# Two chunked scans: the step scaling of the turned channels given to ScalarE, and the first scan's gate moved ahead of the carry

## What is computed

```python
def step(h, inp):                       # per position t and head (16 heads of 64 channels)
    h = h * dA_t + (dt_t * x_t) * B_t   # dt: the step, one number per position and head
    return h, einsum('bhpn,bn->bhp', h, C_t)
y = ys + D_param * xh                   # the skip
y = y * silu(z)                         # the gate
y = y * rsqrt(mean(y * y) + 1e-5) * rms_w ; return y @ out_proj_w.T
```

## Time and profile before

| | us |
|---|---|
| median of 3 runs | 4476.42 (4476.28 to 4478.08) |
| the profiled execution | 4481.21 |
| its span in the profile | 4479.5 |
| TensorE busy in the span | 4064.1 (91%) |
| VectorE busy | 3152.3 (70%) |
| ScalarE busy | 1652.2 (37%) |
| GpSimd busy | 1034.0 (23%) |

### The profile page before, as it was taken

One profiled execution on the slowest core, in us unless ns is written; L12 is line 12 of the kernel. 1 busy time (PEld: TensorE's weight loads), 2 busy tenths in 40 slices (PEclk: granted clock), 3 DMA queues, 4 the chain that ended last, 5 costly groups with the idle time before them and its releaser, 6 DMA issues. The chain is left out here.

```text
span 4479.5 us, 71612 instructions
## 1 busy us (share of the span) xinstructions
PE 4064.1 (91%) x26200; PEld 3023.7 (68%) x26200; DVE 3152.3 (70%) x6457; ACT 1652.2 (37%) x3472; POOL 1034.0 (23%) x597
## 2 busy tenths in 40 slices
PE   6999999998799999999778888898898799999999
PEld 5767676765566666666466676576576478787877
DVE  5787878774489999899657647657557566666664
ACT  3434343432333333343237537447357311111111
POOL 0333434343055555555500000000000000000000
PEclk8999999999899999999889999999999899999999
DMA  2110111001201111111143142242341310101000
GB/s 107 37 37 29 38 42 39 28 35 39 86 26 51 44 39 45 51 44 37 40 175 100 62 142 84 92 134 62 117 126 50 121 34 24 34 22 36 27 26 19
DMA packets 150049, 266.40 MB, mean 59 GB/s; under 512 B 30276, under 2 KB 36424, under 8 KB 149704
## 3 DMA queue, kind: packets, MB, share of 16 engines
q1 hardware_dynamic: 149704, 261.83, 17.5%
HBM read 164.88 MB, written 88.34 MB: 57 GB/s over the span
## 5 line engine op out<-in xcount | busy, mean ns | idle before, releaser
L1866 DVE TENSOR_REDUCE xa_mn<-xa_s 128x1 f32<-128x896 f32 (+7 forms) x512 | 373.0, 751 | 135.8 <-PE xa_s L1961 134.8
L1781 ACT ACTIVATE xa_src<-xa_s,xa_mn 128x896 f32<-128x896 f32 (+7 forms) x512 | 377.7, 740 | 231.6 <-DVE xa_mn L1866 230.3
L1967 PE MATMUL xa_gen<-xa_ident,xa_src 128*128 128x128 f32 x2304 | 310.2, 278 | 53.3 <-ACT xa_pT L1790 26.3
L73 PE MATMUL ff_wb<-ff_w_hi,ff_st_hi 128*128 128x512 f32 x768 | 323.8, 422 | 10.4 <-DVE ff_parts L2472 10.4
L940 DVE SCALAR_TENSOR_TENSOR mb_cv<-mb_xc,mb_cw,mb_cv 128x256 f32<-128x256 f32 x432 | 310.8, 773 | 31.9 <-ACT mb_xc L746 27.8
L1728 POOL TENSOR_TENSOR xa_res<-xa_res,xa_bor 128x512 f32<-128x512 f32 x32 | 40.5, 1270 | 1244.7 <-DMA xa_res<-after_mamba_dram 1244.7
L74 PE MATMUL ff_wb<-ff_w_hi,ff_st_lo 128*128 128x512 f32 x768 | 311.9, 406 | 0.0
L75 PE MATMUL ff_wb<-ff_w_lo,ff_st_hi 128*128 128x512 f32 x768 | 311.1, 405 | 0.0
L1967 PEld LDWEIGHTS xa_gen<-xa_ident,xa_src 128*128 128x128 f32 x2304 | 251.1, 143 | 75.1 <-ACT xa_src L1781 59.5
L1309 PE MATMUL mb_ib<-mb_wc,mb_yT 128*128 128x512 f32 x512 | 262.6, 661 | 1.8 <-DVE mb_y L1078 1.0
L2240 POOL TENSOR_TENSOR ff_mixed<-ff_at,ff_rw 128x1024 f32<-128x1024 f32 x32 | 60.9, 1904 | 875.3 <-DVE ff_at L2500 875.3
(11 more groups left out here) (494 smaller groups left out, 11031.7 us busy)
## 6 DMA issues: line engine op xcount, KB each, us to landing
xa_qa<-xa_q_dram SPq DMA_DIRECT2D x384, 64.0 KB, 2.0
xa_q_dram<-xa_kq SPq DMA_DIRECT2D x32, 512.0 KB, 2.8
xa_k_dram<-xa_kq SPq DMA_DIRECT2D x32, 512.0 KB, 2.8
xa_ka<-xa_k_dram SPq DMA_DIRECT2D x192, 64.0 KB, 2.0
xa_st<-xa_k_dram SPq DMA_DIRECT2D x192, 64.0 KB, 2.0
mf_xg<-in_x_dram SPq DMA_DIRECT2D x16, 512.0 KB, 5.1
turned_dram<-mf_xt_hi SPq DMA_DIRECT2D x16, 512.0 KB, 2.7
turned_dram<-mf_xt_lo SPq DMA_DIRECT2D x16, 512.0 KB, 4.0
```

The source lines that it names most:

```text
L73: nc.tensor.matmul(out, w_hi, x_hi, start=first, stop=False)
L1781: a_.activation(pq[:, hh, 0:w], s1[g, i, hh][:, 0:w], ACT.Exp, scale=-1.0, bias=mn[:, i % 2, hh:hh + 1], accum_out=sums[:, i // QT, i % QT ...
L1866: v_.tensor_reduce(mn[:, i % 2, hh:hh + 1], s1[g, i, hh][:, 0:(i + 1) * P], AX.X, ALU.min).then_inc(mx_ready.sem, 1)
L1967: last = tr(ps[:, n * P:(n + 1) * P], pq[:, hh, j * P:(j + 1) * P], ident[:])
```

## The change

In both scans GpSimd's product of `xtok` and the steps goes away. A new step `scaled` on ScalarE makes `xdt` with one operation per head, sixteen per chunk, each 128 x 64 with the head's step as a per-partition scale. It stands right behind `turn` and ahead of `front` or of the rest of `back`. GpSimd's skip product now waits for it. In the first scan's even turns `gate` comes ahead of `carry`.

```diff
                 if 0 <= n - 1 < N:
                     yield "turn", n - 1
+                if 0 <= n + 1 < N:
+                    yield "scaled", n + 1
                 if n % 2 and 0 <= (n + 3) // 2 < NGF:
                     yield "front", (n + 3) // 2
...
                 if -1 <= n < N:
                     yield "mixed", n
+                if -1 <= n < N and not backward and n % 2 == 0:
+                    yield "gate", n
                 if 0 <= n < N:
                     yield "carry", n
...
-                if -1 <= n < N:
+                if -1 <= n < N and (backward or n % 2):
                     yield "gate", n
...
             def inputs(c):
                 (r, t), b = ring(c), c % 2
-                wait(pool, dt_ready, c // GT)
...
-                g_.tensor_tensor(heads(xdt[:, b]), heads(xtok[:, b]), bcast(dt[:, r, t, :], 2, HP), ALU.mult)\
-                    .then_inc(xdt_ready.sem, 1)
                 wait(pool, xdt_ready, c)
                 g_.tensor_tensor(heads(xtok[:, b]), heads(xtok[:, b]), bcast(dsk[:], 2, HP), ALU.mult).then_inc(skip_ready.sem, 1)
...
+            def scaled(c):
+                (r, t), b = ring(c), c % 2
+                wait(act, dt_ready, c // GT)
+                if backward:
+                    wait(act, dt_loaded[c // GT % 2], c // GT // 2)
+                wait(act, xtok_ready, 2 * c + 1)
+                wait(act, intra_full, NQ * (c - 1) - 1)
+                if c >= 2:
+                    wait(act, xw_ready, outer(c - 2) - int(final(c - 2)))
+                if c == 1:
+                    act.wait_ge(half_ready, 2 * KD)
+                for h in range(NH):
+                    cols = slice(h * HP, (h + 1) * HP)
+                    last = a_.activation(xdt[:, b, cols], xtok[:, b, cols], ACT.Identity, scale=dt[:, r, t, h:h + 1])
+                last.then_inc(xdt_ready.sem, 1)
```

More of the change, by code:

```diff
@@ L858, in _ @@
             run({"split": split, "consts": consts, "combine": combine, "xT": turn_in, "front": front, "back": channels, "sums": sums, "inputs": inputs,
-                 "turn": turn, "square": square, "tanh": front_tanh, "silu": silu, "mixed": mixed, "output": output})
+                 "turn": turn, "scaled": scaled, "square": square, "tanh": front_tanh, "silu": silu, "mixed": mixed, "output": output})
         @block.vector
```

## The result

The changed kernel takes 4497.47 us (median of six runs, 4486.17 to 4499.47), the kernel before 4478.09 on the same chip: a ratio of 1.004 [1.0027, 1.0053]. So the change costs 19 us: slower, as forecast, but by half of the 38 us that were forecast. The profiled execution of the changed kernel took 4497.97 us, 16.8 more than that of before.

What follows compares the result with a forecast made beforehand. The scans were taken as bound by TensorE's work plus its stalls. +91 - 22 - 33 - 28 + 30 = +38 us on the profiled 4481.2 gave 4519, and 4514 as median of runs; range 4450 to 4576.

Steps and rivals of the forecast that it cites:

- The new operations: ScalarE's sixteen scaled operations: 354 ns each, one starting every 0.25 us, 4.0 us put into its turn, bounds 2.6 and 5.7.
- +91: Both scans: TensorE's first z product waits for ScalarE's bank copies, 2.27 or 2.23 us in even turns, 0.8 in odd.
- +121 and -83: Forecast losses, +91 for z product stalls and +30 for clock, against savings of 22 (gate), 33 (state) and 28 (clock).
- The gate: First scan, even turns: gate ahead of carry ends the transposes' 24.4 us wait, about 2.4 returning as later state: -22 us.
- The state: Second scan: without GpSimd's product the taps shorten, VectorE waits for TensorE, state waits fall to 0.74 each: -33 us.
- The clock: Half speed behind the second scan's long stalls goes, -28 us; the new 2.2 to 2.3 us stalls cost +30 us.
- I take half: Clock loss behind the 30 new even-turn stalls, 2 us each: none makes 0, all make 60, so +30 us.
- The even exchange: Rival: the new 2.2 us z product stalls don't lower the clock; +8 us, 4484, counted as no change; chance 0.17.
- VectorE stays late: Rival: second scan's taps don't shorten, so the 33 and 28 us don't come back; +99 us, 4575; chance 0.05.
- Dear operations: Rival: ScalarE's operations don't overlap, 5.7 us put in, stalls of 4.0 and 2.5; +172 us, 4648; chance 0.08.
- The faster case: Rival: ScalarE's short operations start closer together, 0.16 us apart giving -57 us, 4419, or 0.21 giving 4448; chance 0.15.

Runs made afterwards that it cites:

- skip-twice kernel: The changed kernel with the sixteen operations directly behind `inputs`, and GpSimd doing the skip product twice in a row: 4482.44 us, 1.0009 against the kernel before.
- The ratio of 0.9823: The changed kernel with the sixteen operations directly behind `inputs` in turns with channel units, behind `turn` in the others: 4398.43 us, 0.9823 against the kernel before.

## Why the forecast had the sign right and the size wrong

**The stalls of the first z product: right in kind, 18 us too large.** The step that failed is "The new operations", and with it the term **+91**. "One starts every 0.25 us, and sixteen put 4.0 us into ScalarE's turn": one starts every 0.239 us, and 3.68 are put in. Three parts of that price were a little too high: the short operation takes 257 ns with a number as its scale where the nearest row had 262; two of them overlap by 348 - 239 = 109 ns where I had 100; and the first overlaps the end of `yT`, which I had not counted. The pointer's 92 ns were right (91). The estimate by the Trainium skill ("ScalarE: Activation LUTs", section on what ACT_TABLE_LOAD costs), 0.24 us apart and 3.8 put in, agrees with the run in the spacing (0.239) and comes nearer to the 3.68 than my 4.0; I had set it aside for a row that was some 20 ns dearer. With the slack that was read the earlier trace rows, 3.68 make stalls of 1.95 and 0.47; measured are 2.00 and 0.52, so the slack was right to 0.05. The odd stall shows in 13 turns of a scan, not in 15. 2 x (15 x 2.00 + 13 x 0.52) = **+73**. The net of +38 was a small difference of large terms, +121 and -83, so 18 us in one of them halve it. The prediction named a spacing under 0.24 us as a sign of being wrong, and 0.239 is one, if only just.

**The gate: right in size.** -22 forecast; by itself -20 in the time and -22.4 in the first scan. That 2.4 of the 24.4 come back as a later state is not what happened: the waits for the state rise by 0.3, and with the gate moved alone 3.4 us of its own wait are left, in three turns. In the changed kernel none is left.

**The state: right.** 53.3 - 21.4 = -32, forecast -33, through the chain that was named: taps of 6.65 us (forecast 7.3), then VectorE waiting for TensorE.

**The clock: near in both terms, in one of them by luck.** Half speed loses about half of its time. In the second scan it fell by 75.1 - 37.5 = 37.6 us, so 19 come back net; in the first it rose by 37.5, so 19 are lost. The sum is 0; the forecast was -28 + 30 = +2. In the first scan the clock fell behind 12 of the 15 even stalls, in the second behind 7. One fall is 3.4 us at half speed, 1.7 lost: 19 of 1.7, or +32, where I had 15 of 2; the falls behind the long state waits, 61 us at half speed, are gone, -31 where I had -28. "I take half" was the middle between none and all of the 30, worked out from no row, and that 19 is near 15 is luck. The number also differs between executions: the changed kernel's six runs go from 4486.17 us at a granted clock of 0.965 to 4499.47 at 0.961.

**The sum with the measured sizes** is +73 - 20 - 32 + 0 = +21. The two scans together are 31.3 - 10.2 = 21.1 longer. That it fits this closely is in part chance, for by scan it misses by some 5 us each way: 73/2 - 20 + 19 = 36 against 31.3, and 73/2 - 32 - 19 = -15 against -10.2. Where these 5 us come from is open. Of the 4.3 us that are gone outside the scans, 3.7 lie ahead of the first z product of either scan, where the first chunk is prepared; no run was made for them.

**The rivals.** The even exchange gave the nearest time (4484), but by a cause that did not hold: it had no falls of the clock, and there were 19. "VectorE stays late" is refuted by the taps, and in the skip-twice kernel one sees what it would have cost. Dear operations did not come. The faster case put its turning point at 0.22 us apart with falls of the clock (by its own sum it is 0.21: 53 - 83 + 30 = 0), and the measured 0.239 stands on the other side: with twelve operations at the place, which is as much put in as sixteen 0.18 us apart, the kernel is 1.1% faster than before.

**What the forecast missed of the change:** it treats the place as given and costs the stall there. The ratio of 0.9823 shows that the same work on ScalarE was worth 80 us together with the gate, and that its place behind `turn` cost about 100.

## What to carry to other kernels

When work moves to an engine that is mostly idle, find what stands behind it in that engine's order and how much slack that has; the share of busy time (37% here) says nothing of it. If a row of short operations overruns the slack by little, a cheap remedy is to move some of them a step earlier, to where the idle time is, and the price of a stall includes the clock that it costs. And work that nobody waits for can still set the pace of an engine beside it: give it a second copy and see who slows down.

## What was not expected of the hardware

That the clock falls behind some of the z products' stalls was forecast; which of them it falls behind is the surprise. Such a stall is 1.75 us of idle time in the first scan, no longer than the gate's of 1.74 in the kernel before, after which the clock stayed at 1.00 through the steady part. The granted clock of the changed kernel over the 8 us behind an even turn's z stall of the first scan, of one of the second, and of another of the first (at 581.0, again 1.75 us):

```profile
515.50:523.50 8.00, 8.00 (x42) 7.08 (x41) 7.28 (x17) 1.65 (x4) 0.00 (x0) 0.79 0.06 20
1628.30:1636.30 8.00, 8.00 (x39) 7.04 (x40) 6.54 (x16) 2.99 (x7) 2.37 (x2) 0.79 0.15 52
582.00:590.00 8.00, 8.00 (x52) 7.09 (x51) 7.28 (x17) 2.03 (x5) 0.00 (x0) 1.00 0.07 22
```

0.79 is some 3.4 of 8 us at 1.2 GHz; the third stall, as long as the first and at the same place of a turn, was followed by no fall. In the kernel with `scaled` alone both kinds of stall stand in the first scan, and the half-speed time is the same 51.2 us as without the gate's: the clock fell behind 10 of the 15 z stalls and behind one of the gate's, of 1.92 us, as long as the one in the earlier trace rows behind which it stayed at 1.00. The second scan of that kernel has the code of the changed kernel's and the same even stalls, of 1.64 to 1.74 us; yet the clock fell behind 11 of the 15 there and behind 7 in the changed kernel. Over the whole second scan of the changed kernel, and then of that with `scaled` alone:

```profile
1223.00:2238.00 1015.00, 948.03 (x5074) 667.58 (x5072) 814.03 (x1552) 503.58 (x1266) 478.96 (x268) 0.98 0.13 42
1250.00:2271.00 1021.00, 955.41 (x5074) 675.50 (x5072) 813.91 (x1552) 502.91 (x1266) 476.88 (x267) 0.97 0.13 42
```

So neither the length of the idle time nor its place in the code decides alone; the moment at which a stall comes must count too. What it is about the moment, no run was made to tell. In the kernel with four operations early the z stalls of 0.8 us had no fall.
